# A graph network kernel: POOL waits for the landing two back in front of every gather of the attention and relation loops

## The reference

```python
h = relu(layernorm(x)); x = x + L0(h)   # mean of edge attributes per source, then a two-layer MLP
h = relu(layernorm(x)); x = x + L1(h)   # mean of h[src] per dst, [h, mean] @ W, relu
h = relu(layernorm(x)); x = x + L2(h)   # graph attention with 8 heads, then a feed-forward part
h = relu(layernorm(x)); x = x + L3(h)   # relations
```

```python
# L2: attention (src and dst with one self loop per node added)
e = leaky_relu(a_src[src] + a_dst[dst], 0.2)
e = exp(e - segment_max(e, dst)[dst]); alpha = e / segment_sum(e, dst)[dst]
out = segment_sum(alpha[:, :, None] * h[src], dst)
# L3: one of three weight matrices per edge
msg[k] = x[src[k]] @ W_rel[type[k]].T
out = (x @ W_self.T + b).at[dst].add(msg); out = relu(out)
```

## Time and profile before

| | |
|---|---|
| timed runs | 9649.23, 9646.02, 9627.27 us (median 9646.02) |
| profiled execution, its span from first to last instruction | 9754.5 us |
| granted TensorE clock, mean over the span | 0.759 of full speed |
| busy: PE, PEld, DVE, ACT, POOL | 68%, 47%, 64%, 50%, 55% |
| attention loop, first gather of the block to last L2318 | 3679.7 to 6713.7 us |
| relation loop, first to last gather | 7024.7 to 9642.7 us |

### The profile page before, as it was taken

How to read it: one execution, slowest core, us unless ns; L and a number is a source line. 1 busy time by engine, 2 the same in 40 slices (tenths; PEclk the granted TensorE clock), 3 DMA queues, 4 the chain that set the end, 5 groups by cost and what they waited for, 6 DMA issues and landing times. The chain is left out here.

```text
span 9754.5 us, 145261 instructions
## 1 busy us (share of the span) xinstructions
PE 6607.5 (68%) x38830; PEld 4546.4 (47%) x38831; DVE 6236.8 (64%) x16834; ACT 4860.4 (50%) x11241; POOL 5337.6 (55%) x4893
## 2 busy tenths in 40 slices
PE   6988888875888852555555555557767666666665
PEld 3545545544777741445454444557533333333332
DVE  7999999986888832666676666668633333333333
ACT  5877777754777721333333333333334444444442
POOL 5888888873555545455555545551344444444444
PEclk9999999987888955555655555555577788888777
DMA  5444444441111112222222222222111111111111
GB/s 120 73 75 70 72 75 70 72 76 41 21 20 21 21 41 38 44 43 45 45 46 44 45 43 45 44 45 75 51 38 43 45 46 46 46 46 43 41 41 46
DMA packets 626461, 487.11 MB, mean 50 GB/s; under 512 B 513289, under 2 KB 530030, under 8 KB 616344
## 3 DMA queue, kind: packets, MB, share of 16 engines
q0 software_dynamic: 281600, 185.95, 15.9%
q1 hardware_dynamic: 342455, 293.43, 10.2%
q10 hardware_dynamic: 2304, 6.55, 0.3%
HBM read 303.43 MB, written 182.13 MB: 50 GB/s over the span
## 5 line engine op out<-in xcount | busy, mean ns | idle before, releaser
L1600 POOL DMA_INDIRECT tile_rows<-att_row_table,src_by_tile x1620 | 1528.4, 943 | 1413.6 <-PE banks L2269 763.7
L3027 POOL DMA_INDIRECT rows_l<-relation_table,idx x1302 | 1246.4, 957 | 1390.5 <-ACT idx L2967 1012.3
L976 POOL DMA_INDIRECT acc<-val,idx x1116 | 1722.6, 1544 | 378.9 <-issue 319.9
L3232 PE MATMUL banks<-h_parts,dense_onehot 128*128 128x448 bf16 x6510 | 1511.3, 383 | 553.0 <-issue 518.2
L2269 PE MATMUL banks<-tile_rows,prob 128*128 x4032 | 910.4, 402 | 1386.3 <-ACT prob L2210 595.5
L747 PE MATMUL banks<-part 128*128 128x490 bf16 (+1 forms) x7440 | 1569.6, 366 | 217.9 <-DVE part L830 209.8
L2269 PEld LDWEIGHTS banks<-tile_rows,prob 128*128 128x128 f32 x4032 | 831.8, 307 | 1480.6 <-issue 1480.3
L3232 PEld LDWEIGHTS banks<-h_parts,dense_onehot 128*128 128x128 bf16 x6510 | 643.0, 103 | 1334.6 <-issue 854.1
L747 PEld LDWEIGHTS banks<-part 128*128 128x128 bf16 x7440 | 694.3, 97 | 996.0 <-DVE part L830 270.4
L3144 DVE TENSOR_TENSOR h_nodes<-banks,dense_mask_j 128x448 f32<-128x448 f32 x310 | 192.9, 622 | 1476.3 <-remote 910.1
L2210 ACT COPY prob<-banks 128x1024 f32<-128x1024 f32 x252 | 255.0, 1012 | 1307.8 <-DMA quad_sums<-run 1076.4
(11 more groups left out here) (449 smaller groups left out, 12370.0 us busy)
## 6 DMA issues: line engine op xcount, KB each, us to landing
src_rows<-src_by_column SPq DMA_DIRECT2D x63, 1152.0 KB
piece_sums<-kept_l SPq DMA_DIRECT2D x252, 264.0 KB
running_sums<-run SPq DMA_DIRECT2D x62, 832.0 KB
attr<-in_edge_attr SPq DMA_DIRECT2D x61, 624.0 KB
tile_rows<-att_row_table,src_by_tile POOLq DMA_INDIRECT x1620
rows_l<-relation_table,idx POOLq DMA_INDIRECT x1302
dense_code_rows<-src_by_column SPq DMA_DIRECT2D x62, 320.0 KB
acc<-val,idx POOLq DMA_INDIRECT x1116
```

Of the source, the lines that this page charges most:

```text
L976: e.indirect_dma_start(acc_d[k], bass.IndirectOffsetOnAxis(ap=idx[h][:, r:r + 1], axis=0), val[h][:, r, :], None, compute_op=ALU.add).then ...
L1600: e.indirect_dma_start(to, None, hx_d, bass.IndirectOffsetOnAxis(ap=src_col[:, t:t + 1], axis=0))\
L3027: e.indirect_dma_start(g[h][:, r, :], None, y3_d, bass.IndirectOffsetOnAxis(ap=idx[h][:, r:r + 1], axis=0))\
L3232: last = e.matmul(ps[4 + b][:, 0:WJ], hot[h][:, k, m * P:(m + 1) * P], parts3[:, n, k * WJ:(k + 1) * WJ], start=(k == 0 and n == 0), stop= ...
```

## The change

In the attention loop each of the four semaphores becomes a pair, for the even and the odd gathers of a unit. Every gather from the second unit of the loop on waits for the landing of the gather two before it: the third to eighth of a unit for one of the same unit, the first and second for the last two of the unit before. The wait for the unit four back is dropped. SP's signal waits for both halves. The relation loop gets the same: two semaphores a buffer, a wait from the third gather of a half on, and ScalarE waits for both counts. The gathers before the loop that bring the semaphores to their starting count become eight instead of four. To have semaphores left, those of layer 0 are noted in a list and given back at the end of that layer.

```diff
-            s_attr = [sem(f"l0_attr{h}") for h in range(2)]
+            l0_sems = []
+            s_attr = [sem(f"l0_attr{h}", l0_sems) for h in range(2)]
...
-            retire(retired0)
+            retire(l0_sems + retired0)
...
-        s_tile = [sem(f"l2_tiles{k}") for k in range(TSEMS)]
+        s_tile = [[sem(f"l2_tiles{k}_{n}") for n in range(2)] for k in range(TSEMS)]
         EARLY = 1
 
-        def gather_tile(e, t, to, k):
+        def gather_tile(e, t, to, k, n):
             e.indirect_dma_start(to, None, hx_d, bass.IndirectOffsetOnAxis(ap=src_col[:, t:t + 1], axis=0))\
-             .then_inc(s_tile[k], 16)
+             .then_inc(s_tile[k][n], 16)
...
-                    for k in range(TSEMS):
-                        gather_tile(e, k, gathered[:, TRING - 1, k, :], k)
+                    for k in range(2 * TSEMS):
+                        gather_tile(e, k, gathered[:, TRING - 1, k, :], k // 2, k % 2)
                     for g in range(EARLY):
                         for r in range(QUAD):
-                            gather_tile(e, g * QUAD + r, gathered[:, g, r, :], g)
+                            gather_tile(e, g * QUAD + r, gathered[:, g, r, :], g, r % 2)
...
+                    def landed(g):
+                        return 8 * QUAD * (g // TSEMS) + 16
+
                     for g in range(EARLY, TU):
                         if g >= TRING:
                             if g % GATES == 0:
                                 gates = loaded(gate[0:1, g:g + GATES], mybir.EngineType.Pool, 1, NQ)
                             e.wait_ge(s_sum, (gates[g % GATES] & 511) + SUMS0)
                             e.sem_inc(s_pace, 1)
-                        if g >= TSEMS:
-                            e.wait_ge(s_tile[g % TSEMS], 16 * QUAD * (g // TSEMS) + 16)
-                            e.sem_inc(s_pace, 1)
                         for r in range(QUAD):
-                            gather_tile(e, min(g * QUAD + r, T - 1), gathered[:, g % TRING, r, :], g % TSEMS)
+                            if r > 1:
+                                e.wait_ge(s_tile[g % TSEMS][r % 2], landed(g) + 16 * (r // 2))
+                                e.sem_inc(s_pace, 1)
+                            elif g > EARLY:
+                                e.wait_ge(s_tile[(g - 1) % TSEMS][r], landed(g - 1) + 8 * QUAD)
+                                e.sem_inc(s_pace, 1)
+                            gather_tile(e, min(g * QUAD + r, T - 1), gathered[:, g % TRING, r, :], g % TSEMS, r % 2)
...
                         for k in range(TSEMS):
-                            e.wait_ge(s_tile[k], (((n + (TSEMS - 1 - k)) >> 2) << 7) + 16)
-                            e.sem_inc(s_pace_sp, 1)
+                            for half in range(2):
+                                e.wait_ge(s_tile[k][half], (((n + (TSEMS - 1 - k)) >> 2) << 6) + 16)
+                                e.sem_inc(s_pace_sp, 1)
...
-            s_rows = [sem(f"l3_rows{h}", l3_sems) for h in range(2)]
+            s_rows = [[sem(f"l3_rows{h}_{n}", l3_sems) for n in range(2)] for h in range(2)]
+            LANDED = [-(-NGA // 2), NGA // 2]
...
-                        e.wait_ge(s_rows[h], i * 16 * NGA + 16 * NGA)
+                        for n in range(2):
+                            e.wait_ge(s_rows[h][n], i * 16 * LANDED[n] + 16 * LANDED[n])
...
                             for r in range(NGA):
+                                if r > 1:
+                                    e.wait_ge(s_rows[h][r % 2], i * 16 * LANDED[r % 2] + 16 * (r // 2))
+                                    e.sem_inc(s_pace, 1)
                                 e.indirect_dma_start(g[h][:, r, :], None, y3_d,
                                                      bass.IndirectOffsetOnAxis(ap=idx[h][:, r:r + 1], axis=0))\
-                                 .then_inc(s_rows[h], 16)
+                                 .then_inc(s_rows[h][r % 2], 16)
```

More of the change, by code:

```diff
@@ L640, in build @@
             src_z = src0f[:, 0:T].rearrange("p (h r) -> p h r", r=HALF)[:, :, HS:HALF]
-            s_attr = [sem(f"l0_attr{h}") for h in range(2)]
+            l0_sems = []
+            s_attr = [sem(f"l0_attr{h}", l0_sems) for h in range(2)]
             s_stage, s_psrc, s_eq, s_sum, s_val, s_hot, s_hist, s_dup, s_tgt, s_vfree, s_acc = (
-                sem(f"l0_{n}") for n in ("staged", "src_rows", "equal", "summed", "values", "onehots", "hist",
+                sem(f"l0_{n}", l0_sems) for n in ("staged", "src_rows", "equal", "summed", "values", "onehots", "hist",
                                          "dup", "targets", "val_free", "pace"))
             s_high, s_left, s_spread, s_z, s_dig, s_digits = (
[L646 to L651, removed]
+                sem(f"l0_{n}", l0_sems) for n in ("high_parts", "rests", "spread", "z_added", "digits_staged", "digits"))
+            s_add = [sem(f"l0_acc{k}", l0_sems) for k in range(NACC)]
+            s_init, s_tail, s_pack = (sem(f"l0_{n}", l0_sems) for n in ("init", "tail", "packed"))
+            s_away, s_gap = (sem(f"l0_{n}", l0_sems) for n in ("digits_negated", "digit_distances"))
+            s_srow = [sem(f"l0_src_rows_loaded{h}", l0_sems) for h in range(2)]
+            s_turn, s_turnc, s_turnst = (sem(f"l0_{n}", l0_sems) for n in ("src_turned", "src_turned_copied", "src_turned_stored"))
             assert TT * P >= T + HALF > (TT - 1) * P and 12 < TT < 17 and TT * P <= HS * P
```

## The result

The kernel after takes **9343.1 us** (9341.0 to 9350.1, 4 runs) against 9640.2 for the kernel before (9627.3 to 9649.2, 4 runs): ratio 0.9691, 95% interval 0.9677 to 0.9705. It is 297 us faster, where 686 were forecast (from 9646). The time lies in the range, near its upper end.

The account below looks back on a forecast made before the run. It took TensorE stalls of about 12 to 15 us in long runs of unwaited POOL gathers as the bound. Span 9754.5 - 248 (attention) - 436 (relation) = 9070, less 108.5 gives 8960 us; range 8690 to 9420.

Parts of the forecast that it names:

- The stalls that go: Attention and relation loops: TensorE stalls, seen as VectorE's 877.3 and 908.9 us of "remote" waits, vanish or become negligible.
- The waits that come: POOL gathers slow from 1.25 us to 1.72 in attention (bounds 1.25 to 1.88) and 3.42 a pair in relation.
- The pace in relation: Relation loop: ten pairs of 3.42 us plus 1.25, about 35 us a burst against 42.4 before, saving 436 us.
- The 108.5 us: Whole kernel: timed median 9646.0 us lies this far below the profiled span 9754.5; subtracted from the forecast span of 9070.
- What is late next: Both loops: POOL becomes the bound, with compute following the gathers; saves 248 us in attention, 436 in relation.
- A: Both loops: the wait is free, POOL keeps 1.25 us a gather, compute becomes the bound; about 7790 us; chance 0.06.
- B: Both loops: stalls last until bursts end, and bursts grow by 6.3 and 8.8 us; 10,650 us, slower; chance 0.14.
- D: Both loops: no change, longer bursts and shorter holes cancel; chance 0.03.
- the prediction's 0.20: Summed chance of the two rivals said to lie outside the range 8690 to 9420: compute bound 0.06, slower 0.14.
- C: Only one loop relieved, or holes halved in both: 9210 us (relation alone) to 9400 (attention alone); chance 0.08.
- its reading of the earlier trace: Attention and relation loops: TensorE loses about 12 to 15 us in every long run of unwaited POOL gathers.
- the rule weighed in the prediction: DMA never contends with compute engines except through the VectorE/GpSimd port; then limiting transfers returns none of the 684 us.

Follow-up runs that it names:

- met-wait kernel: Kernel before, with an already met wait (staged indices) ahead of each relation gather, layer 0's semaphores handed back: 7566.5 us (ratio 1.0002); later 9771.6 us (1.0133).
- occasion 3: Timing session where TensorE nearly stops in places: before 9654.6 us, its unchanged repeat 9646.1, after 9333.5, only relation waits 9267.7, attention store doubled 9806.9.
- before again: The kernel before, unchanged, timed and profiled once more beside itself: 9646.1 us against 9654.6.
- occasions 5 and 6: Two timing sessions without TensorE holes: before 7568 and 7564 us; landing waits only after every 8 or 7 gathers 8234 and 8237; after 9114 in the second.
- the rests: Against before: POOL waits for the last landing only after every 8 gathers (attention) or 7 (relation): 8963.7 us beside 9783.2 with holes; 8234 and 8237 without.
- occasions 2 and 7: Two timing sessions, both recorded on chip 14: kernel before took 7566 us in the first, without TensorE holes, and 9783 in the second, with them.

## Why the prediction was right or wrong

*The stalls that go: right, on occasions that have them.* "Remote" in front of both steps is gone in the profile after.

*The waits that come: wrong in attention, and this is the step that failed.* It took 1.72 us a gather, "a little above". Measured 1.89, a little above the upper bound of 1.88. 1608 gathers by the 0.17 us are 273 us, and with them the forecast's own arithmetic gives a last step at 3679.7 + 1608 x 1.89 + 20 = 6739 us against 6713.7 before: nothing saved. The reason was in the kernel, not in the rows of the middle layer: the store of the sums meets a gather once in eight. With POOL as the bound this is not chance. A step starts when its rows land and the store follows: in the trace after, all 243 stores that are issued between the loop's first and last gather stand behind the first, second or third gather of a group (97, 102 and 44), while the 238 of the met-wait kernel's unbraked loop fall on all eight (24 to 49 each). In place of 248 us gained, the attention waits lost 66 us: 314 of the missing 365 (9333.5 less 9267.7 against -248).

*The pace in relation: nearly right.* 35 us a period were forecast, (9252.7 - 35 - 7008.3) / 61 = 36.2 came. A pair took 3.50 us on average for the forecast's 3.42, and the forecast had rounded its 35.4 down. (Its sum for the period before, as written, gives 42.5 and not 42.4, which is worth 6 us.) 387 us against 436: 49 more of what is missing (all from occasion 3, where the whole gain is 321 us and 365 are missing from 686).

*The 108.5 us* between the profiled and the timed runs carried over harmlessly into the level, but not as a property of the kernel: the profile of before again has a span of 9642.5 beside a median of 9646.1. The first profile was a long execution: its relation loop takes 2618.0 us against 2598.6 in the second profile, its attention loop 3015.9 against 2979.1. The forecast took its gains from these longer loops, so up to 56 us of them were not to be had in a usual execution; this overlaps with the two shortfalls above and is no third one.

*What is late next: right.* POOL, in both loops; 948 and 909 us of VectorE waiting for a TensorE that waits for rows.

*The rivals.* A (7790, compute bound) fell: the wait is not free. A gather lands 2.13 us after its start in the relation loop of after, less than two unwaited starts, but the gather that waits for it starts another 1.10 us later (medians). Holes gone at 1.25 us a gather does exist, at 7566 us, but in the kernel before on an occasion without holes, and there no wait is wanted. B (10,650) fell: with the waits there is no long hole. Its place and price were wrong, yet its sign is what occasions 5 and 6 would give. D (no change, about 9646) lies outside the stated range like A and B, which the prediction's 0.20 leaves out; it did not come either, though for the attention loop alone it describes what happened: the holes gone, the gathers slower by as much. The mechanism on the slower side that was not listed is the simplest: no holes, and waits that only cost, +1550 us. C fell for both loops together, though its relation-alone figure, 9210, is near the measured 9268: one loop was relieved and the other was not.

*What was missing altogether* is that the holes come and go with the occasion. Three timed runs within 22 us of each other and one trace can't show that. The prediction called its reading of the earlier trace rows "a correlation within one trace, not a proof"; its chances didn't follow that caution.

## What to carry to other kernels

A brake on one engine costs its full price wherever it acts and brings a gain only where the disturbance is present, so measure a kernel on several occasions before you brake it; here the rests stand at 0.917 with holes and 1.089 without, the relation waits alone at 0.960 and 1.077, both waits at 0.967 and 1.205. A landing wait is priced by the slowest transfer that meets it in lockstep, not by the mean landing nor by a quiet loop's rows: look for the store that the same step triggers. And add up all waits in front of a line before and after, whatever they are put down to: in attention 877 us "remote" against 948 us for TensorE said at once that nothing was gained, but in relation the two largest rows, 909 and 909, would have said the same and been wrong, for 508 us of other waits had mostly gone.

## What the runs showed of the hardware

- The same program took 7566 or 9646 us by occasion, steady within each. It isn't a fixed property of a chip: occasions 2 and 7 are recorded for the same one, with before at 7566 and 9783. Which of the chip's cores ran, and what else ran beside it, is not on record; neither was tried, so the cause of the difference is open.
- On the occasions with holes TensorE issues single matmuls 2.1 to 2.8 us apart while POOL starts a gather every 1.25 us. The transfers take no longer. Part 3 of the page (packets, MB, share of 16 engines), before again and then met wait on occasion 2:

```profile
q0 software_dynamic: 281600, 185.95, 15.4%
q1 hardware_dynamic: 342455, 293.43, 10.3%
```

```profile
q0 software_dynamic: 281600, 185.95, 20.3%
q1 hardware_dynamic: 342455, 293.43, 13.3%
```

  15.4% of 9642.5 us are 1485 us and 20.3% of 7561.5 are 1535; 993 and 1006 for the other queue. A relation gather lands after 2.13 us (median) in both. This agrees with the rule weighed in the prediction (the Trainium skill, "SBUF — State Buffer", section "Who interferes with whom"): nothing here shows that the moving of data stops TensorE. In a hole TensorE waits for nothing that the profile names; its next instruction starts late.
- TensorE isn't the only engine that is slowed. SyncE's MOVE in front of its load of the codes, in before again and then in the met-wait kernel of occasion 2 (durations in ns, min/median/max):

```profile
L3043 SPq MOVE dense_code_rows<-src_by_column x58: 3/684/1382, 6974.0 to 9408.9; - x58
```

```profile
L3047 SPq MOVE dense_code_rows<-src_by_column x58: 29/29/29, 5861.5 to 7356.5; - x58
```

  The same register instruction has a median of 684 ns in place of 29; in the hole shown above it starts at 8018.35 and takes 0.70 us. Not every instruction is affected: SyncE's store of the sums in the same loop (L3048) keeps its 351 ns.
- The relation loop's holes are not filled by loading instructions by DMA, as far as the profile lists it. The profile lists such transfers as a kind of their own, "instruction", 102 of them in each of these two executions. Between 7130 and 9490 us of before again, which is nearly the whole relation loop, there are none:

```profile
q0 software_dynamic: 38144, 39.14, 8.8%
q1 hardware_dynamic: 16176, 66.39, 8.0%
```

  What holds the instructions up instead is open.
- Not all of the difference between occasions is in the two loops: the first attention gather is at 3584 to 3639 us with holes and at 3391 to 3399 without.
- A wait that is already met costs nothing on one occasion (ratio 1.0002) and 128 us on another (1.0133, two runs; VectorE's "remote" before the dense tile 1026 us in place of before's 762 us of occasion 3). Why is open.
